# A graph, attention and expert layer on one core: additions moved into layer 2, weight splits, slot places and the final planes reordered

## The reference

```python
xn = layernorm(x)
gcn = lambda h, W, b: segment_sum((h @ W)[src] * norm[:, None], dst) + b    # with self loops
x = x + gcn(relu(gcn(xn, W1, b1)), W2, b2) + mix(xn)
x = x + moe(layernorm(x))
# mix: linear attention, 4 heads; rmsnorm(out @ w_out + b_out, g_out) + xn
# moe(t): t + sum over the 2 best of 8 experts of share * (gelu(t @ w1[e] + b1[e]) @ w2[e] + b2[e])
```

## Time and profile before

| what | us |
|---|---|
| median of 3 runs (lowest, highest) | 791.93 (786.92, 793.68) |
| the profiled execution's own time | 797.36 |
| span of the profiled execution, first to last instruction | 795.6 |
| busy: TensorE, VectorE, ScalarE, GpSimd | 596.3, 511.6, 347.0, 134.5 |
| mean granted TensorE clock (1 is 2.4 GHz) | 0.872 |

### The profile page before, as it was taken

One profiled execution on the slowest core, in us unless ns is written; L12 is line 12 of the kernel. 1 busy time (PEld: TensorE's weight loads), 2 busy tenths in 40 slices (PEclk: granted clock), 3 DMA queues, 4 the chain that ended last, 5 costly groups with the idle time before them and its releaser, 6 DMA issues.

```text
span 795.6 us, 13909 instructions
## 1 busy us (share of the span) xinstructions
PE 596.3 (75%) x5198; PEld 526.3 (66%) x5198; DVE 511.6 (64%) x1077; ACT 347.0 (44%) x623; POOL 134.5 (17%) x132
## 2 busy tenths in 40 slices
PE   0699582862999999999599999988850399999400
PEld 0254241752999999997499999888750399998300
DVE  6767998468999999954841111396761177877424
ACT  0026464280777777750131111322320399898200
POOL 1000000000000000000000000007786256655500
PEclk9879986795999999999799999998855599999855
DMA  7999999002134444000027686302332345554295
GB/s 181 263 283 283 284 282 345 4 1 93 64 158 207 208 208 208 2 1 1 1 86 327 270 350 236 134 1 69 82 86 78 89 124 155 157 147 136 53 248 188
DMA packets 80159, 121.17 MB, mean 152 GB/s; under 512 B 8574, under 2 KB 68771, under 8 KB 78430
## 3 DMA queue, kind: packets, MB, share of 16 engines
q1 hardware_dynamic: 70621, 107.03, 44.4%
q0 software_dynamic: 9472, 13.27, 5.2%
HBM read 50.00 MB, written 72.21 MB: 154 GB/s over the span
## 4 chain that ended last, share of the span: by engine, by line
PE 52%; DVE 24%; DMA 7%; issue 5%; ACT 4%; POOL 3%; SPq 1%; DVEq 1%; another core or an unknown queue 0%; ACTq 0%; POOLq 0%
PE psB L1218 20%; DVE hot L677 7%; PE psB L1370 4%; PE psD L1274 3%; PE psC L1124 3%; PE psC L1218 3%; PE psA L1136 3%; DMA back<-expert_out 3%; POOL expert_slots L568 3%; PE psD L1136 2%; DMA acc<-in_x_dram 2%; PE psC L1382 1%; PE psD L1382 1%; PE psA L1358 1%; DVE qkv L726 1%
## 5 line engine op out<-in xcount | busy, mean ns | idle before, releaser
L1218 PE MATMUL psB<-hs,counts 125*128 125x256 f16 x1600 | 210.8, 275 | 3.3 <-DVE hs L791 2.7
L1218 PEld LDWEIGHTS psB<-hs,counts 125*128 125x128 f16 x1600 | 173.0, 140 | 4.6 <-issue 2.8
L677 DVE TENSOR_TENSOR hot<-iota_j,places 128x2048 bf16<-128x2048 bf16 x128 | 155.2, 1223 | 15.4 <-PE psA L1136 9.8
L560 POOL IOTA row_of<- 128x25 f32 x1 | 0.2, 237 | 503.5 <-PE psC L1218 503.5
L1413 ACT CAST counts<-psA 128x1000 f16<-128x1000 f32 x64 | 63.3, 989 | 39.6 <-PE psA L1136 39.6
L1136 PE MATMUL psA<-hot 128*128 128x125 bf16 x512 | 50.8, 224 | 36.8 <-DVE hot L677 34.0
L574 POOL DMA_INDIRECT expert_out<-y,to_row x64 | 67.2, 1050 | 61.3 <-DVE y L1060 48.5
L568 POOL DMA_INDIRECT expert_slots<-rows,place x50 | 63.1, 1263 | 50.3 <-issue 48.2
L1136 PEld LDWEIGHTS psA<-hot 128*128 128x128 bf16 x512 | 39.2, 100 | 47.0 <-DVE hot L677 36.2
L1413 ACT CAST counts<-psD 128x1000 f16<-128x1000 f32 x64 | 63.6, 993 | 13.9 <-PE psD L1136 13.9
L851 DVE TENSOR_TENSOR sum_both<-psB,sum_both 128x256 f32<-128x256 f32 x32 | 13.5, 421 | 74.6 <-ACT sum_both L1475 74.6
(11 more groups left out here) (284 smaller groups left out, 1076.2 us busy)
## 6 DMA issues: line engine op xcount, KB each, us to landing
expert_slots<-zeros SPq DMA_DIRECT2D x8, 3536.0 KB, 30.2
kept_counts<-counts SPq DMA_DIRECT2D x6, 4000.0 KB, 11.8
counts<-kept_counts SPq DMA_DIRECT2D x6, 4000.0 KB, 13.0
xs<-expert_slots SPq DMA_DIRECT2D x32, 272.0 KB
back<-expert_out SPq DMA_DIRECT2D x5, 1120.0 KB
w_raw<-in_L_ffn_w_dram SPq DMA_DIRECT2D x2, 2048.0 KB, 7.9
acc<-in_x_dram SPq DMA_DIRECT2D x1, 2800.0 KB
out_dram<-acc SPq DMA_DIRECT2D x5, 560.0 KB
```

Source lines behind the costliest of these rows:

```text
L677: v.tensor_tensor(hot[:, slot].rearrange("p g w n s -> p (g w) n s"), iota_j[:, :, :].unsqueeze(1).to_broadcast([P, 2 * pairs, P, PAIR]), ...
L1218: m = pe.matmul(sum_bank(g, d), counts5[0:PT, buf, a, d, :], hs2[0:PT, a, :, :].rearrange("p q f -> p (q f)"), start=a == 0 and first, sto ...
```

## The change

- `add_xn` and `add_b2` leave the projections, and `add_mix` the end of the attention. Two vectors are computed early, `acc_scale` 0 = 1 + rstd and 1 = -mean * rstd, so that x + xn = x * scale0 + scale1 and `xn` isn't read for it. In layer 2, chunks 0 to 4, VectorE does after the three groups of chunk i, for block i and node by node: `scale_mix`, `add_mix` (acc * scale0 + mix), `add_b2` (acc + scale1 + b2).
- w2 is loaded behind w1. ScalarE rounds w1 and w2 after the last block's router. VectorE takes w1's low part after the table of tiles and after GpSimd has issued its last scatter (a memset with a semaphore says so), and w2's low part in the expert loop, at t = -1.
- `slot_places(c - 1)` stands right behind `router(c - 1)`. On TensorE `merge_transposed(c + 1)` is cut in three: one node, `logits(c - 1)`, two nodes, `ranks(c - 1)`, two nodes.
- At the end both planes of a block are added as it lands, and it can be stored.
- `b2_all` and `gout_all` move to another place in SBUF, since they live longer.

```diff
@@ SP
             for k in range(SPILLED):
-                if k == 1:
-                    sp.wait_ge(acc_mixed, C)
-                    sp.dma_start(w2_raw[...], moe_w2...).then_inc(in_w2, 16)
                 sp.wait_ge(counts_ok, UNITS * (k + 1))
...
             sp.dma_start(w1_raw[...], moe_w1...).then_inc(in_w1, 16)
+            sp.wait_ge(acc_mixed, SLOTS)
+            sp.dma_start(w2_raw[...], moe_w2...).then_inc(in_w2, 16)
             sp.dma_start(b2_rows[...], moe_b2...).then_inc(in_b2, 16)
@@ GpSimd, behind the 50 scatters
+            pool.memset(issued[:, :], 0.0).then_inc(spread_issued, 1)
@@ VectorE
+                    v.tensor_scalar(acc_scale[0:PT, 0, :], rstd[0:PT, :], 1.0, None, ALU.add).then_inc(acc_scale_ok, 1)
+                    v.scalar_tensor_tensor(acc_scale[0:PT, 1, :], mv[0:PT, :, 0], -1.0, rstd[0:PT, :], ALU.mult, ALU.mult).then_inc(acc_scale_ok, 1)
...
+            def scale_mix(c):
+                for n in range(W * c, W * c + W):
+                    v.scalar_tensor_tensor(mix[0:PT, n, :], mix[0:PT, n, :], mnorm[0:PT, n:n + 1], gout_all[0:PT, :], ALU.mult, ALU.mult).then_inc(mix_scaled, 1)
+            def add_mix(c):
+                for n in range(W * c, W * c + W):
+                    v.wait_ge(mix_scaled, n + 1)
+                    v.scalar_tensor_tensor(acc[0:PT, n, :], acc[0:PT, n, :], acc_scale[0:PT, 0, n:n + 1], mix[0:PT, n, :],
+                                           ALU.mult, ALU.add).then_inc(acc_scaled, 1)
             def add_b2(c):
+                for n in range(W * c, W * c + W):
+                    v.wait_ge(acc_scaled, n + 1)
+                    v.scalar_tensor_tensor(acc[0:PT, n, :], acc[0:PT, n, :], acc_scale[0:PT, 1, n:n + 1], b2_all[0:PT, :],
+                                           ALU.add, ALU.add).then_inc(acc_mixed, 1)
...
                 hot_unit(unit % 2, UNIT * unit)
-                if unit < C:
-                    add_xn(unit)
-                elif unit < 2 * C:
-                    add_b2(unit - C)
...
             v.wait_ge(norm_ok, 1)
-            for c in range(C):
-                add_mix(c)
...
                     for i, k in enumerate(SECOND_ORDER):
-                        if i == 1:
-                            v.wait_ge(w_hi_ok, 1)
-                            v.tensor_tensor(w2_lo[:], w2_raw[:], w2_hi[:].bitcast(F32), ALU.subtract).then_inc(w_lo_ok, 1)
                         for g in range(SG):
                             sums_add(CH + i, g)
                             sums_low(k, CH + i, g)
+                            if i < C:
+                                (scale_mix, add_mix, add_b2)[g](i)
...
-            v.wait_ge(w_hi_ok, 2)
-            v.tensor_tensor(w1_split[:, 0], w1_raw[:], w1_split[:, 1].bitcast(F32), ALU.subtract).then_inc(w_lo_ok, 1)
...
                 if c >= 1:
                     router(c - 1)
+                    slot_places(c - 1)
...
                 v.tensor_tensor(a, a, tok[:, :, 0:DIM], ALU.add).then_inc(acc_tok_ok, 1)
-                if c >= 1:
-                    slot_places(c - 1)
...
             v.wait_ge(table_ok, 2)
+            v.wait_ge(spread_issued, 1)
+            v.wait_ge(w_hi_ok, 1)
+            v.tensor_tensor(w1_split[:, 0], w1_raw[:], w1_split[:, 1].bitcast(F32), ALU.subtract).then_inc(w_lo_ok, 1)
             for t in range(-2, MOE_TILES):
...
+                if t == -1:
+                    v.wait_ge(w_hi_ok, 2)
+                    v.tensor_tensor(w2_lo[:], w2_raw[:], w2_hi[:].bitcast(F32), ALU.subtract).then_inc(w_lo_ok, 1)
...
                 v.tensor_tensor(a, a, back[0:PT, c, 0], ALU.add).then_inc(first_back_ok, 1)
-            for c in range(C):
-                a = acc_v[0:PT, c]
                 v.wait_ge(first_back_ok, c + 1)
                 v.tensor_tensor(a, a, back[0:PT, c, 1], ALU.add).then_inc(out_ready, 1)
@@ TensorE
                     token_transposes(c - 1)
-                    logits(c - 1)
-                if c < C - 1:
-                    merge_transposed(c + 1)
-                if c >= 1:
-                    ranks(c - 1)
+                for part, nodes in enumerate((range(0, 1), range(1, 3), range(3, W))):
+                    if c < C - 1:
+                        merge_transposed(c + 1, nodes)
+                    if c >= 1 and part < 2:
+                        (logits, ranks)[part](c - 1)
...
-            pe.wait_ge(w_lo_ok, 2)
+            pe.wait_ge(w_lo_ok, 1)
...
+                    if t == 0:
+                        pe.wait_ge(w_lo_ok, 2)
@@ ScalarE
-            act.wait_ge(xn_free, C)
-            act.wait_ge(acc_xn_ok, C)
...
-                    act.wait_ge(in_w2, 16)
-                    act.copy(w2_hi[:], w2_raw[:]).then_inc(w_hi_ok, 1)
...
-            act.wait_ge(in_w1, 16)
-            act.copy(w1_split[:, 1], w1_raw[:]).then_inc(w_hi_ok, 1)
...
             odds_exp(C - 1)
+            act.wait_ge(in_w1, 16)
+            act.copy(w1_split[:, 1], w1_raw[:]).then_inc(w_hi_ok, 1)
+            act.wait_ge(in_w2, 16)
+            act.copy(w2_hi[:], w2_raw[:]).then_inc(w_hi_ok, 1)
```

41 lines of the change are left out of this document (17 added, 24 removed).

## The result

| | before | after |
|---|---|---|
| median of the runs (lowest, highest) | 792.8 (786.92, 795.96), 4 runs | 757.38 (754.86, 760.83), 4 runs |
| ratio, with its 95% interval | | 0.9555 (0.9525 to 0.9585) |
| profiled execution, its span | 797.36, 795.6 | 756.59, 754.8 |
| mean granted TensorE clock | 0.872 | 0.896 |

The forecast was 757.8 us.

The account below looks back on a forecast made before the run. The prediction saw a row of stages with different bounds (VectorE, TensorE, GpSimd, ScalarE, DMA). Its terms, -9.6 - 19.2 + 0 + 1.5 - 3.1 - 3.7 = -34.1 us, took the 791.93 us median to 757.8; own range 751 to 762, wider range 751 to 767.

Parts of the forecast that it names:

- 1, the projections: Projections: ten xn and b2 additions leave VectorE, six of them on the chain; -9.6 us, bounds -7 to -10.5.
- 2, the gap: Before layer 1: scaling and adding leave, so TensorE starts earlier and keeps its clock; -19.2 us, range -17.4 to -20.
- The clock's share: Behind the gap before layer 1: no half-speed stretch of TensorE after a long rest; 1.8 us of the gain.
- A rest of 2.9 us should not bring this: Before layer 1: the shorter TensorE rest leaves its clock up; if not, the part is -17.4 us.
- 3, layer 2: Layer 2, chunks 0 to 4: VectorE's moved additions, 2.07 us a set, are hidden; 0 us, bounds 0 to +3.
- rival (c): Layer 2: VectorE becomes the bound of chunks 0 to 4, its additions exceeding the chunk; +46, so 804 us; chance 0.01.
- 4, the weights: Node blocks and experts' start: w1's low part hidden, w2's delays the first `h_lo`; +1.5 us, bounds 0 to +3.
- Kept to the end: Expert loop: the +1.5 us lost at its start stays, as neither engine has slack in the loop.
- 5, places and order: Node blocks: earlier places and TensorE's new order bring the first scatter forward, GpSimd not waiting again; -3.1 us, bounds -5 to +1.
- The collision: Node blocks: block 1's addition to acc falls among the scatters and lengthens one; +1.2 us, cancelling two waits.
- 6, the planes: End: stores stand behind the loads and start as they end, 13 us from about 779; -3.7 us, bounds -4.5 to +1.
- Rival (a): Small costs all fall due: stores and loads share engines, the clock falls in both rests; -26.3, so 765.6 us; chance 0.17.

Follow-up runs that it names:

- a0_after_again: The changed kernel measured once more with no edit; 765.37 us, ratio to the kernel before 0.9606.
- e78: The changed kernel with the additions put back in the projections and before layer 1, out of layer 2; 800.39 us, ratio 1.0089.
- e4: The changed kernel with five more 125x256 instructions behind each of VectorE's 15 sets in layer 2; 774.32 us, ratio 0.9761.
- b0: The kernel before the change, run once more with no edit; 791.76 us in one run.
- e9: The changed kernel with the end as before: all first-plane additions, then all second ones; 772.6 us, ratio 0.9671.
- e2: The changed kernel with w2's low part right behind w1's, ahead of the expert loop; 763.09 us, ratio 0.9584.
- c1: The changed kernel with one-input scalings of acc in the node blocks and w2's low part ahead of the expert loop; 757.6 us, ratio 0.9538.
- e5: The changed kernel with the places behind the rows and the addition to acc again, TensorE's new order kept; 767.31 us, ratio 0.9665.
- e6: The changed kernel with TensorE's old order, the places kept right behind the router; 769.1 us, ratio 0.9667.
- e1: The changed kernel with the stores waiting until the last load of planes has landed; 767.07 us, ratio 0.9629.

## Why the prediction was right, and where its terms were not

The total held: -34.1 us forecast, -35.4 by the medians of the first measurement, -31 by a0_after_again's ratio (0.9606 of 792.8 is 761.6, also within the range). That the first measurement came within 0.4 us of 757.8 is luck, that both lie within the range is not. Four terms held, one of them (4) on weak evidence, and two missed, in opposite directions.

**1, the projections (-9.6).** -9.25 in the first trace, 9.33 back in e78; over the eleven profiles -7.3 to -9.5 against the first profile of before, whose own second profile is 1.3 us earlier there. That six of the ten additions were links, and what each gave back, came from the replay of VectorE's order; counting all ten would have said 14. TensorE's rest came as forecast (2.76 us for 2.9) and left its clock alone in nine of eleven profiles; in a0 and e4 it didn't, at 1.9 and 1.5 us, near the 2 us that the prediction had for this.

**2, the gap (-19.2).** -20.15 from the projections' end to the start of layer 2; the end of the range forecast was -20. The next to come late was ScalarE's `counts`, as read. The clock's share came back in e78 (1.77 us). But "A rest of 2.9 us should not bring this" held in seven of eleven profiles only; in the other four the clock fell again, at 1.4 to 1.6 us, between TensorE's resuming and layer 2. Taken as in the first trace, the part is -17.1 to -20.2 over the eleven, -19.3 in the mean, so the first profile shows its better end.

**3, layer 2 (0).** VectorE's sets cost nothing. The 1.3 us that layer 2 lost stand in its first chunk, where TensorE's clock, at 1.2 GHz behind the rest between the layers, came back later: 0.68 from 370 to 375, 2.2 us behind its first product, where before the change 400 to 405, 2.8 us behind it, has 1.00. Layer 2 took 110.7 to 110.9 us in four profiles (before, b0, e9, e2) and some 112 in the other nine that double no set, in e78 without any addition there. The sum was right, but one line of its working was wrong: "Beyond 8.2 - 1.7 = 6.5 us a set would hold up TensorE." That counts each set against its own bank. The load of a chunk counts, as rival (c) had it: (13.65 - 3.2) / 3 = 3.5 us a set is the limit, an estimate from e4's chunks; e4 itself shows that 4.63 us a set, below 6.5, holds TensorE up. At 2.06 the margin was there by either rule.

**4, the weights (+1.5).** The start came as forecast: the first `h_lo` 1.3 us late against the transposes as TensorE sees it (8.65 to 9.93), w1's part hidden. "Kept to the end" looked wrong in the first trace, where the last down product was 34.5 us early after 32.4 at the first. Over ten profiles it looks right, 118.2 against 116.4 before and 116.7 in e2 and c1; this rests on means of lengths that scatter by 3.7 us, with only two profiles in each of the other groups, and is not shown.

**5, places and order (-3.1).** The step that failed is "GpSimd needs 16.1 us per block, so it is not left waiting again". The first scatter gained more than forecast, 3.0 to 3.9 us (27.3 to 28.2 after 31.2), and needed both halves, as e5 and e6 show. The collision cost less: the first block's pair gave 1.67 us instead of 2.38, since that addition had begun before the scatter, and the sum of all was 2.4 us against 3.5 before. But the waits came back. From layer 2's end to the last scatter the seven profiles with unedited node blocks and scatters (after, a0, e9, e1, e2, e4, e78) have 106.4 to 113.2, mean 110.2; the two of before have 112.6 and 110.0, mean 111.3. So the part is worth about 1 us by the means, which so few profiles don't tell from nothing, and the first profile's 6.2 was its luckiest case. What came in its place are the stalls of TensorE's and VectorE's issue: in four of the seven (a0, e9, e1, e2) GpSimd waits 2.3 to 2.6 us for places at two blocks of five, in e78 2.95 us at one.

**6, the planes (-3.7).** The order was read rightly, "four stores stand behind them and start as they end": e1 and a0 show the stores moving next to nothing until the fourth load has landed. The step that failed is the price, "So the 13 us start at about 779". The 13 us of before were the time of stores that began on an empty queue (12.5 in e9, 13.1 in e1). Stores in line need 7.7 to 7.9 us behind the last landing, since they first fill the stretch that the last load leaves idle and then run on without a start. Against e9's 15.5 the part is worth some 7.7 us. By the length of the whole stage it is 4.8 to 8.6 (44.3, 44.3 and 42.8 in before, e9 and b0, 35.7 to 38.0 in the others), since the loads themselves take 27.7 to 30.1 us. The first profile had the slowest loads, so it shows 6.3. Rival (a)'s sharing, by which the last load would land later, did not come: it landed 28.5 us behind the first issue in a0 and in e1. The loads of after and c1 (30.1 and 29.7) were slow already up to the fourth landing, when no store had moved anything to speak of; why is not known.

So the nearly exact total has some 2 us too much from part 5 and some 4 too little from part 6 in it, the first profile alone would have misjudged 2, 4 and 5, and the length of the end alone would have misjudged why 6 paid.

## What to carry to other kernels

Work that fills an idle engine inside a stage held by another one is free as long as the idle engine's whole load per period stays below the period; the slack behind a single item is not the measure. Where two edits must both be in place before a date moves, each alone measures as nothing, so test them apart and together. A measured figure that fits one theory does not prove it: e1's +5.2 us looked like stores running beside loads, and only the bytes moved in each stretch showed that they had stood in line. And before a stage's length from one profile is used, look at how it scatters: here what lies ahead of layer 2, layer 2, the scatters and the experts varied by 5.1, 1.1, 6 and 3.7 us between executions of the same code, in the last three more than the edits in them were worth.

## What was not expected of the hardware

- Stores issued 11 to 22 us behind the first load of the same queue moved next to nothing until the fourth of five loads had landed (5.6 to 5.7 MB in all, with and without them), and did not delay the loads. Then they filled what the last load left idle (326 GB/s against 148) and ran on at 304 GB/s, where stores on an empty queue took 243.
- A scatter issued while VectorE ran a two-input subtraction of 4.43 us took 5.11 us: it ends 1.07 us behind the subtraction, as those beside additions of 1.49 us do. With one-input scalings beside it, it takes 1.19 to 1.30.
- Behind one and the same rest of TensorE of 2.97 to 2.99 us the granted clock fell in four executions (0.66 to 0.71 over the next 5 us) and stayed full in seven; not explained.
- Between the 39th and the 40th scatter GpSimd rests 3.54 to 3.86 us in every profile, before and after, wherever the blocks' places stand by then; not explained.
- The stalls in the node blocks ("issue" on TensorE in steps of 0.3 to 0.5 us, "remote" on VectorE and ScalarE of 1.3 to 12.1 us); not explained.
